# A sort and a convolution block on one core: x added by TensorE, shorter first runs, other places for the sort's steps

## The reference, cut to what matters

```python
x = x + conv(layernorm(x))        # 1x1 step, 3x3 step with relu, and a last 1x1 step of 128 outputs; conv adds its own input
t = tokens(x)
t = t + ffn(layernorm(t), edge_index)
```

```python
e = leaky_relu(a_src[src] + a_dst[dst])
ee = exp(e - segment_max(e, dst)[dst])
agg = segment_sum(h[src] * (ee / segment_sum(ee, dst)[dst]), dst)
```

## Time and profile before

| | |
|---|---|
| median of three runs | 2209.75 us (2204.56 to 2211.97) |
| the profiled execution's own time | 2207.2 us |
| its span, first to last instruction | 2205.3 us |
| mean granted clock of TensorE, share of full | 0.771 |
| TensorE busy | 1222.1 us, 55% of the span |
| VectorE busy | 1649.0 us, 75% |
| ScalarE busy | 773.1 us, 35% |
| GpSimd busy | 1156.2 us, 52% |

### The profile page before, as it was taken

The page is one execution under the profiler, slowest core; times in us unless marked ns, Lnnn a source line. Parts: engine busy times, 40 slices in busy tenths (PEclk is TensorE's granted clock), DMA queues, the critical chain, the costliest instruction groups (busy, mean ns, idle before and its releaser), DMA issues.

```text
span 2205.3 us, 17414 instructions
## 1 busy us (share of the span) xinstructions
PE 1222.1 (55%) x5234; PEld 557.3 (25%) x5234; DVE 1649.0 (75%) x3153; ACT 773.1 (35%) x1294; POOL 1156.2 (52%) x1167
## 2 busy tenths in 40 slices
PE   5888789785349988400701084373727272727361
PEld 2233343334223433200300032131313131313120
DVE  7987988999769999999394443848484848484757
ACT  5866567362225555300300042131313131313131
POOL 2000000000037777777777777777777777777750
PEclk9998889895569999855855597695959586868676
DMA  9202111213416222211321134243535352525261
GB/s 330 100 1 71 14 2 39 8 39 8 45 33 104 74 72 73 53 14 41 79 42 18 26 83 154 69 158 84 158 84 158 77 165 67 175 60 175 56 165 44
DMA packets 142665, 177.41 MB, mean 80 GB/s; under 512 B 64170, under 2 KB 115308, under 8 KB 132972
## 3 DMA queue, kind: packets, MB, share of 16 engines
q1 hardware_dynamic: 85014, 88.59, 14.3%
q0 software_dynamic: 40768, 42.44, 12.3%
q10 hardware_dynamic: 16790, 45.29, 5.4%
HBM read 99.82 MB, written 76.40 MB: 80 GB/s over the span
## 4 chain that ended last, share of the span: by engine, by line
POOL 51%; issue 17%; DVE 15%; PE 10%; ACT 4%; DMA 1%; POOLq 0%; SPq 0%; DVEq 0%; ACTq 0%
POOL KC L544 45%; PE hidden_out L711 3%; PE Z L711 3%; POOL KC L643 3%; DVE KC L1334 2%; DVE KC L1335 2%; PE MB L725 2%; POOL XG L591 1%; DVE KA L1334 1%; DVE KA L1335 1%; ACT ARENA_Y L900 1%; ACT ARENA_A L965 1%; DVE XG L1996 1%; PE TA L680 1%; PE MB L806 1%
## 5 line engine op out<-in xcount | busy, mean ns | idle before, releaser
L544 POOL DMA_INDIRECT KC<-node_dram,KB x1026 | 1025.5, 1000 | 930.0 <-DVE KB L1558 617.7
L779 PE MATMUL hidden_out<-XT,W 128*128 128x512 f32 x512 | 281.0, 654 | 433.9 <-ACT ARENA_A L1057 433.0
L784 PE MATMUL hidden_out<-ARENA_A,W 128*128 128x512 f32 x512 | 266.1, 645 | 24.9 <-ACT ARENA_A L1057 24.9
L1057 ACT ACTIVATE ARENA_A<-hidden_out,b1c 128x512 f32<-128x512 f32 x256 | 174.2, 687 | 243.5 <-PE hidden_out L779 242.9
L779 PEld LDWEIGHTS hidden_out<-XT,W 128*128 128x128 f32 x512 | 95.3, 204 | 583.0 <-ACT ARENA_A L1057 460.0
L806 PE MATMUL MB<-KA,ident 128*128 128x512 f32 x320 | 166.3, 673 | 63.0 <-DVEq L1824 63.0
L1803 DVE TENSOR_TENSOR KB<-KC,MB 128x320 f32<-128x320 f32 x66 | 29.2, 484 | 187.6 <-DMA KC<-payload,slot_idx 187.0
L1132 ACT ACTIVATE TA<-KB 128x320 f32<-128x320 f32 x64 | 26.0, 438 | 378.2 <-DVE KB L1813 378.1
L1060 ACT ACTIVATE ARENA_A<-hidden_out,b2c 128x512 f32<-128x512 f32 x128 | 88.0, 687 | 187.0 <-PE hidden_out L784 187.0
L1996 DVE SCALAR_TENSOR_TENSOR XG<-XT,KB,XG 128x128 f32<-128x128 f32 x512 | 144.1, 347 | 3.7
L784 PEld LDWEIGHTS hidden_out<-ARENA_A,W 128*128 128x128 f32 x512 | 98.3, 206 | 182.5 <-ACT ARENA_A L1057 103.2
(11 more groups left out here) (413 smaller groups left out, 2233.9 us busy)
## 6 DMA issues: line engine op xcount, KB each, us to landing
ye_dram<-ARENA_D ACTq DMA_DIRECT2D x32, 1024.0 KB, 4.1
XT<-ye_dram SPq DMA_DIRECT2D x32, 1024.0 KB, 11.6
KC<-node_dram,KB POOLq DMA_INDIRECT x1026
payload<-XT SPq DMA_DIRECT2D x1, 11520.0 KB
payload<-KC SPq DMA_DIRECT2D x115, 90.0 KB, 1.9
XG<-x_dram SPq DMA_DIRECT2D x32, 256.0 KB, 9.2
out_dram<-XG ACTq DMA_DIRECT2D x32, 256.0 KB, 2.7
KA<-in_L_ffn_edge_index_dram SPq DMA_DIRECT2D x1, 2048.0 KB, 14.2
```

The source lines that it names most:

```text
L544: pool.indirect_dma_start(row_buf[h][:, t, :], None, node_dram, bass.IndirectOffsetOnAxis(ap=KB[:, col:col + 1].bitcast(I32), axis=0)).the ...
L779: last = pe.matmul(PF[i % 2][:, :], W1[:, m // 2, (m % 2) * P:(m % 2) * P + P], XT[:, n * CHUNK:(n + 1) * CHUNK], start=True, stop=True)
L784: last = pe.matmul(PF[i % 2][:, :], W2[:, 2 * m + kk, :], HH[:, 2 * m + kk, :], start=kk == 0, stop=kk == 1)
L1057: act.activation(HH[:, m, :], PF[i % 2][:, :], ACT.Gelu, bias=b1c[:, m:m + 1]).then_inc(S["hid_out"], 1)
```

## The change

Four things are changed.

1. In `step3`, TensorE adds one more product per chunk into the bank: the identity matrix times the kept x (`x_chunk`), for which it waits on `xres_ready`. ScalarE gets a new function, `add_back`, that copies the bank over the kept x and lets the bank go. It runs in `place_work`, one place behind the products' order, and for the last group in three portions between roots, norms and copies. The addition on VectorE is gone from `residual`.
2. `RUN` is 32 instead of 64. The row is halved when its runs are 32 long; `sort_row` merges from 32 on. `pick_rest` merges to wider runs with every halving (`WIDER`) and needs no copies.
3. The counts of the sort steps in VectorE's queue are others, and a few steps stand between each variance of the second norm and the scale that follows it. Some that stood between the chunks of a residual now stand ahead of it.
4. `evacuate_keys` is gone from ScalarE: VectorE masks the keys out of TensorE's banks itself, three instructions of three blocks each, and GpSimd waits for the last of them.

```diff
-RUN = 64
+RUN = 32
+WIDER = {HALF: RUN, HALF // 2: 2 * RUN, HALF // 4: 4 * RUN}
...
-STEPS_AFTER = ((0, 3, 0, 3, 0, 3, 0, 0), (0, 5, 0, 5, 0, 5, 0, 0), (0, 5, 0, 5, 0, 5, 0, 0), (0, 0, 1, 0, 1, 1, 1, 0))
+STEPS_AFTER = ((0, 0, 0, 0, 0, 4, 0, 0), (0, 0, 0, 0, 0, 3, 0, 0), (0, 0, 0, 0, 0, 6, 0, 0), (0, 0, 1, 0, 1, 0, 1, 0))
...
-            pool.wait_ge(S["sources_ready"], 1)
+            pool.wait_ge(S["sources_ready"], EVACS)
...
                 for t in range(TPC):
                     tok = (c * TPC + t) * P
-                    last = pe.matmul(bank[:, t * P:(t + 1) * P], relu_of[g][:, tok:tok + P], T3[:, :],
+                    pe.matmul(bank[:, t * P:(t + 1) * P], relu_of[g][:, tok:tok + P], T3[:, :],
                                      start=False, stop=True, skip_group_check=True)
-                last.then_inc(S["step3_ready"], 1)
+                pe.wait_ge(S["xres_ready"], g * CHUNKS + c + 1)
+                pe.matmul(bank[:, :], ident[:, :], x_chunk(g, c), start=False, stop=True, skip_group_check=True
+                          ).then_inc(S["step3_ready"], 1)
...
-                    pe.wait_ge(S["keys_evacuated"], n - 1)
+                    pe.wait_ge(S["sources_ready"], n - 1)
...
+            def add_back(g, c):
+
+                j = g * CHUNKS + c
+                act.wait_ge(S["step3_ready"], j + 1)
+                act.activation(x_chunk(g, c), MB[bank_of[(3, g, c)]][:, :], ACT.Copy).then_inc(S["x1_ready"], 1)
...
                 pending_out()
+                done = sum(STEP3_FILL[g][:place])
+                for c in range(done, done + STEP3_FILL[g][place]):
+                    add_back(g - 1, c)
...
                     if place == 4 and g:
                         root2(g - 1)
+                        pending_out()
                         first_norms(2, g - 1)
...
             pending_out()
+            for c in range(4):
+                add_back(GROUPS - 1, c)
             root2(GROUPS - 1)
             for k in range(GROUPS - 1, len(STATS2)):
                 norms(norm_at[(2, GROUPS - 1, 0)] + 2 * (k - GROUPS + 2))
+                if k == GROUPS - 1:
+                    add_back(k, 4)
+                    add_back(k, 5)
                 copies(2)
+                if k == GROUPS - 1:
+                    add_back(k, 6)
+                    add_back(k, 7)
...
-                    dve.wait_ge(S["step3_ready"], j + 1)
-                    dve.wait_ge(S["xres_ready"], j + 1)
-                    tt(x_chunk(g, c), x_chunk(g, c), MB[bank_of[(3, g, c)]][:, :], ALU.add).then_inc(S["x1_ready"], 1)
                     dve.wait_ge(S["x1_ready"], j + 1)
...
-                link(ts(a, a, signs[:, 0:1], None, ALU.mult))
+                link(ts(a, b, signs[:, 0:1], None, ALU.mult))
...
+                n, run = HALF, RUN
+                while n > PICK:
+                    for now in merge_runs(a[:, 0:n], b[:, 0:n], n, run, WIDER[n]):
+                        yield
+                    n, run = n // 2, WIDER[n]
+                    halve(b[:, 0:2 * n], a[:, 0:n], a[:, n:2 * n], run)
                     yield
...
-            sort_steps(8)
+            sort_steps(2)
             scales1(3)
+            sort_steps(23)
+            residual(0)
+            sort_steps(1)
+            scales2(0)
             sort_steps(4)
-            residual(0)
-            scales2(0)
-            sort_steps(5)
             token_stats(4)
-            sort_steps(4)
+            sort_steps(1)
             scales1(4)
-            sort_steps(13)
+            sort_steps(26)
             residual(1)
+            sort_steps(1)
             scales2(1)
-            sort_steps(26)
+            sort_steps(41)
             residual(2)
+            sort_steps(2)
             scales2(2)
-            sort_steps(33)
+            sort_steps(25)
             residual(3)
+            sort_steps(2)
             scales2(len(STATS2) - 1)
...
-                dve.wait_ge(S["keys_evacuated"], EVACS)
-                k = half(KB, 0).bitcast(I32)
-                ts(k, k, (1 << SRC_BITS) - 1, None, ALU.bitwise_and).then_inc(S["sources_ready"], 1)
+                for n in range(EVACS):
+                    dve.wait_ge(S["keys_transposed"], n + 1)
+                    k = BANK_T * n
+                    ts(keys_t[:, k:k + BANK_T, :].bitcast(I32),
+                       TA[n % 2][:, 0:BANK_T * P].rearrange("p (q c) -> p q c", c=P).bitcast(I32),
+                       (1 << SRC_BITS) - 1, None, ALU.bitwise_and).then_inc(S["sources_ready"], 1)
```

More of the change, by code:

```diff
@@ L338, in program @@
             dve_chain split_done
-            rows_sorted rest_placed keys_transposed keys_evacuated keys_stored sources_ready
+            rows_sorted rest_placed keys_transposed keys_stored sources_ready
             hot_ready hist_done hist_tot_ready offsets_ready spread_ready spread_t window_rounds_ready
@@ L1070, in outputs @@
                 act.dma_start(ye_dram[n], YE[n % 2].rearrange("p t n -> p (t n)")).then_inc(ye_stored[n % 2], 16)
[L1072 to L1078, removed]
             def store_rest():
@@ L1094, in _ @@
             act.sem_inc(S["exp_out"], 2)
-            evacuate_keys()
             feed_forward(AHEAD)
@@ L1367, in split_keys, with halve @@
                 yield
-            def halve(src, low, high):
-                runs = src.rearrange("p (g h j) -> p g h j", h=2, j=RUN)
-                to = lambda b: b.rearrange("p (g j) -> p g j", j=RUN)
+            def halve(src, low, high, run=RUN):
+                runs = src.rearrange("p (g h j) -> p g h j", h=2, j=run)
+                to = lambda b: b.rearrange("p (g j) -> p g j", j=run)
                 tt(to(low), runs[:, :, 0, :], runs[:, :, 1, :], ALU.min)
@@ L1412, in pick_rest @@
                 a, b = KA[:, HALF:], KB[:, HALF:]
-                for _ in merge_runs(a, b, HALF, RUN, RUN):
-                    yield
[L1415 to L1429, removed]
+                n, run = HALF, RUN
[4 more added lines that the diff above has]
+                    halve(b[:, 0:2 * n], a[:, 0:n], a[:, n:2 * n], run)
+                    yield
                 dve.sem_inc(S["rest_placed"], 1)
                 picked, other = b[:, 0:n], a[:, 0:n]
-                link(ts(picked, picked, signs[:, 0:1], None, ALU.mult))
+                link(ts(picked, a[:, 0:n], signs[:, 0:1], None, ALU.mult))
                 yield
-                for now in merge_runs(picked, other, n, RUN, n // 2):
+                for now in merge_runs(picked, other, n, run, n // 2):
                     yield
```

## The result

The changed kernel took 2184.03 us (median; 2182.08 to 2185.5) against 2209.31 us of the kernel before in the same comparison: a ratio of 0.9885 (95% interval 0.9871 to 0.99), 25.3 us less. The profiled execution took 2183.02 us, its span is 2181.4.

What follows compares the result with a forecast made beforehand. VectorE was taken to bound the kernel until the first gather, GpSimd's issue afterwards. -10.7 at the sort's end, -0.3 at the hand-over and +0.6 for gathers gave -10.4 us: 2196.8, said as 2197, range 2186 to 2208.

Steps and rivals of the forecast that it cites:

- The bound and the ledger: Until the first gather VectorE sets the pace; its work and waits that go, less waits that come: -10.7 us.
- the work that goes: VectorE before the sort's end: additions of x 22.1 us and sorting 15.3 us go, together 37.4 us.
- the wait ahead of scales1(3): VectorE, after two sort steps instead of eight, waits for ScalarE's square root: new wait of 15.9 us, called certain.
- the three masks: Hand-over from sort to first gather: VectorE masks out of the banks itself, -0.3 us, between -1 and +1.
- the term for TensorE's and ScalarE's lag: Step 3's loop: added products with x make each group 9.5 us longer, ends 7.6 and 15.2; ScalarE's copy adds 0.6.
- The waits of group 1: VectorE's waits for chunks 4 to 7 and the root: 9.4, 2.4, 10.3, 3.6 and 5.5, sum 31.2 us.
- Group 3: Last group: four pairs of chunks, each a round between VectorE, ScalarE and TensorE; new waits 13 to 26, taken as 20 us.
- Half clock everywhere: Rival, TensorE in step 3: products with x take 1.9 us in every place, gain gone, about 2208 us; chance 0.23.
- The larger gain: Rival, waits before the sort's end: low clock shrinks with TensorE denser, gain 16 to 20 us, about 2189; chance 0.08.
- The round trips of the last group: Rival: ScalarE's in-order queue makes the last group wait 40 us instead of 20, about 2220 us; chance 0.09.
- the gain might be the sort alone: Rival: steps between variance and scale may do nothing, leaving only the sort's gain; inside the forecast, no chance of its own.
- The tail: From first gather to end: more sorting of list 1 by VectorE slows GpSimd's gathers, +0.6 us, between 0 and +2.

Runs made afterwards that it cites:

- part 2 alone: The kernel before with only runs of 32 and the new way of picking list 1: 2199.53 us, ratio 0.9965.
- the kernel with all waits filled: The changed kernel with sort steps moved into all of VectorE's long waits: 2145.86 us, ratio 0.973 against the kernel before.
- the first part alone: The kernel before with only x added by TensorE, the bank copied out by ScalarE and VectorE's additions gone: 2202.86 us, ratio 0.9975.

## Why the prediction was wrong, point by point

**What held.** The bound and the ledger; the work that goes (37.4 said, 37.9 measured); the wait ahead of scales1(3) (15.9 and 16.05 us); VectorE's arrival at group 0 (190.5 and 190.75); no wait in group 2; the price of a product with x at the lower level (1.9 said; 1.91 at 198.62 us, with a granted clock of 0.50), although the row that it was read from, at 28.95 us, stands in a stretch for which the profile gives 1.00; the three masks (-0.3 said, within -1 to +1; the way from the sort's end to the gather is 0.2 longer).

**What failed: the term for TensorE's and ScalarE's lag, 9.5 us a group.** It was worked out as 2 x 0.95 in three places and 2 x 1.9 in the fourth. The sum of the first three came out, by luck: the fourth began at 197.25 instead of 191.92, 5.3 us later (5.7 said), but the three took 1.7, 3.2 and 0.1 us longer and not 1.9 each (the rest is a wait). The fourth then added 1.1 instead of 3.8 us: VectorE's last addition had started at 197.08, ScalarE's last copy at 203.46, 6.4 us later instead of 9.5.

```profile
203.46 0.60 ACT L987 ACTIVATE XG<-MB 128x512 f32<-128x512 f32 x1 [2.29 <-PE MB L729]
...
231.23 0.23 ACT L957 ACTIVATE std<-std 128x32 f32<-128x32 f32 x1 [9.32 <-DVE std L1204]
```

The step took the rows at half clock as a property of the fourth place alone and added a product at that price. It had misread the kernel before: there the second and the third place ran at a granted clock of 0.68, and only the first at 1.00. And the runs showed that the product itself takes later rows out of the dip: all of the third place, and the end of the second chunk in the fourth. So group 0 cost 2.4 us of waits and not 6.1. From there the error went on. VectorE gave the statistics of group 3 at the old time (the root ran at 231.23, before at 231.17), not 3.7 us later, and group 1 began with no lag at all. Its last copy started at 333.31, 3.3 us behind the addition of before; the prediction had 13.2. In group 1 the four places had 0.68, 0.51, 0.68 and 0.50 of the clock before and 1.00, 0.62, 1.00 and 0.76 after, and together took 2.1 us longer. The waits of group 1, 7.7, 1.4, 8.5, 1.8 and 4.7, are 24.1 us instead of 31.2, and smaller by less than the lag since VectorE too came 3.7 us earlier. Group 3 cost 16.7 instead of 20: the round trips were there (three waits of 2.0 to 3.6 us for roots), a little shorter. 3.7 + 7.1 + 3.3 is the 14.1. The prediction's own sign of being wrong, a first gather before 612 us, came at 604.2.

**The rivals.** Half clock everywhere, at 0.23, was wrong in its sign: the clock rose, though products with x did take 1.91 us in the first chunks of the second and fourth place. The prediction's "one place in four" is the misreading named above. The rule that was weighed for it, of the Trainium skill, TensorE: Matmul & The Clock Gate, section "A second HAM failure mode: psum-queue depth-cycling", tells of full clock lost between groups of products that cycle through banks. The dips behind the waits are of that kind, but one more product per bank brought the granted clock from 0.86 to 0.91 here. The larger gain, at 0.08, named the very mechanism (low clock shrinks with TensorE denser) and gave it too little, in chance and in size. The round trips of the last group did not come to that price: 16.7 us. Their 40 us had a slip, too: two waits of 6.4 and two of 3.5 in each of four pairs make 79 us; 40 is one of each. That the gain might be the sort alone is answered by part 2 alone, 8.2 of the 25 us.

**The tail.** From the first gather to the end the trace has 1577.2 us instead of 1574.8, 2.4 more; 0.6 was said. About 1 us of it lies ahead of GpSimd's fetch of list 1's windows, while VectorE sorts list 1. From the first gather to that fetch the three kernels with the old sorting of list 1 take 450.6 to 451.0 us, and the seven with the new one whose gather did not wait for node rows 451.6 to 452.0. The other 1.3 come behind it and lie within the spread: there the twelve traces have 1120.3 to 1126.2 us. What sets that spread is open. So are the 7.7 us that the kernel with all waits filled won in the whole tail; 4.1 of them lie ahead of the fetch, and there VectorE was done with the masks 6.5 us ahead of the gather instead of 0.3, but that this is the cause was not tried.

## What to carry to other kernels

Where one engine's queue, written out by hand, sets the pace, a ledger of its work and of its waits, landmark by landmark, gives the end within 2 us once the waits are read from a trace, and foretelling the waits is the hard part. Work that is taken away comes back as waits unless the filling is moved along with it, and here the first part alone kept about a fifth of the work that it took away, the second part about half. Price work added to another engine by the rows of that engine with the work in place, not by adding it to rows of before: a lowered clock behind a wait is not the price of a place. When the waits are filled, ask which other input the consumer needs, since that is the next bound.

## What the runs showed of the hardware that had not been expected

Behind waits of 2.1 to 3.6 us TensorE ran at its lower clock level for 4 to 7 us, or not at all. In the kernel before, a place behind a wait of 2.17 us had a granted clock of 0.68; in the changed kernel the same place, behind 2.49 us, had 1.00. The level fell with the first row behind the wait or only later, as in the changed kernel's fourth place (four products in 1.28 us, then 1.91 for the product with x). One more product with x in each chunk, 32 in all at 1.02 us each at the upper level, cost the kernel 10 us, and the next 32 cost 22.
